# GpSimd waits for gathered rows at every second tile: one core, four graph layers

## The chip, the cores and the metric

The kernel runs on one core of a Trainium2 chip. The metric is the device time of one execution in microseconds, as the median of several runs.

## The reference

Four graph layers follow one another on x (4096 x 128) with one adjacency matrix adj (4096 x 4096, zeros and ones). Before each, x is normalised and floored at zero; the layer's result is added to x. The change lies in the last layer, which is this, cut to its core:

```
z  = leaky_relu(lap_mul(A, h) @ W1 + b1, 0.1)
d2 = sq[:, None] + sq[None, :] - 2.0 * (z @ z.T)
S  = exp(-sqrt(max(d2, 0) + 1e-10) / 2)
S  = where(ranks < 4, S, 0.0)          # the four nearest of each row
A2 = S + A
out = lap_mul(A2, h) @ W2 + b2         # lap_mul(A, x) = d * (A @ (d * x)), d = 1 / sqrt(rowsum(A))
```

So the last product is that of a dense 4096 x 4096 matrix of zeros and ones, plus, for each row, four rows of the same operand with four weights.

## The kernel before

The 4096 rows are 32 tiles of 128 (t), in 8 groups (g) of 4 (q). The kernel is written engine by engine; each engine goes through its list in order and waits on semaphores that count up. A wait holds everything behind it on its engine.

The last stage computes `A2 @ (d * x)` and the output. These are its parts.

TensorE: a tile's product (`product`, L684; matmuls at L680) is 32 matmuls of 128 x 128 weights (the transposed adjacency in 8 bits, tile `panel`, one of four slots q) against 384 bf16 columns (`partsB`), into bank q. It waits for the slot's panel (L687) and for the take of the product four tiles earlier, which frees the bank (L688). The first group is done by `first_products` (L694), all four products side by side. The matmuls of a product follow each other; the last one counts up `s_lprod`.

SP: `load_panel` (L438) loads the slot q of the next group, 512 KB, when the product of that slot is done (L500).

GpSimd: for each tile four gathers (`last_gathers`, L1406, DMA at L1413). One gather is an indirect DMA that fetches 128 rows of 512 bytes from DRAM (`last_features`) by the 128 indices of one column, so 64 KB. Tile t's gathers wait for the take of tile t - 3 (L1408). They land in `near[r * 4 + q]` (in the tile `gath`), with r the parity of the group: eight buffers, each with a semaphore of its own, `s_gath2`. At the third tile of a group the indices of the next group are copied first (`stage_near`, L1402), when the group before is used up (L1421). From the third group on, the buffer of tile t must have been used by tile t - 8 (L1424).

VectorE: `last` (L2193). For each tile it takes the product out of its bank (`take_product`, L1535, a sum over three parts into `agg`, counted by `s_sum`), waits for the tile's four gathers (L2202), and adds the four gathered rows with their weights (three operations at L2204, one at L2207, which counts up `s_gath_used`). After the fourth tile three operations make the output of the group (L2210, L2212, L2216).

ScalarE's queue: it stores each group's output, 256 KB.

An earlier stage, the pooling of the first layer, gathers too: GpSimd issues five gathers for each tile at L1324 and, at the second and fourth tile of a group, waits before them until those of the tile before have landed (`rows_landed`, L1312).

Of the kernel before, what the change touches and what calls it, by code (L numbers as in the profile page):

```python
# [26 lines left out]
G = 4  # L27
# [6 lines left out]
TOP = 4  # L34
# [18 lines left out]
def program(nc, x, adj, w0, b0, w1, w2, w31, b31, w32, b32, out):  # L53
    N, F = x.shape
    NT = N // P
    NG = NT // G
# [5 lines left out]
    with ctx:  # L62
# [3 lines left out]
        def sem(name):  # L66
            return ctx.enter_context(nc.semaphore(name))
# [197 lines left out]
        s_gath2 = [sem(f"nearest_gathered{i}") for i in range(2 * G)]  # L265
# [890 lines left out]
        def _(pool):  # L1156
# [245 lines left out]
            def stage_near(g, r):  # L1402

                pool.tensor_copy(near_idx[r], TI[:, ds(g * G, G), :].rearrange("p q k -> p (q k)")).then_inc(s_idx, 1)

            def last_gathers(g, r, q):  # L1406
                t = g * G + q
                pool.wait_ge(s_sum, 2 * NT + t + 2)  # L1408
                if q == 0:
                    pool.wait_ge(s_idx, NT + g + 1)  # L1410
                pool.sem_inc(waited["pool"], 1)
                for k in range(TOP):
                    pool.indirect_dma_start(near[r * G + q][:, k, :], None, g2_dram,  # L1413
                                            bass.IndirectOffsetOnAxis(near_idx[r][:, q * TOP + k:q * TOP + k + 1], axis=0)
                                            ).then_inc(s_gath2[r * G + q], 16)

            def last_group(g, r, first_pair=False, last=False):
                for q in range(G):
                    if q == 2 and not last:
                        if not (first_pair and r == 0):  # L1420
                            pool.wait_ge(s_gath_used, NT + g * G + 4)  # L1421
                        stage_near(g + 1, 1 - r)
                    if not first_pair:
                        pool.wait_ge(s_gath_used, NT + (g - 2) * G + q + 1 + 4)  # L1424
                    last_gathers(g, r, q)

            stage_near(0, 0)
            last_group(0, 0, True)
            last_group(1, 1, True)
            with pool.Fori(1, NG // 2 - 1) as h:  # L1430
                last_group(2 * h, 0)
                last_group(2 * h + 1, 1)
            pool.wait_ge(s_topi, 2 * NG)
            last_group(NG - 2, 0)
            last_group(NG - 1, 1, last=True)


        @block.vector
# [805 lines left out]
```

## Time and profile before

| what | us |
|---|---|
| time, median of 3 runs | 1810.25 |
| lowest and highest run | 1807.11 and 1820.14 |
| the profiled execution, span | 1795.6 |
| TensorE matmul busy, of the span | 1575.9 |
| GpSimd busy | 570.1 |
| L1413, the 128 gathers of the last stage, GpSimd | 124.4 |

The span reaches from the first to the last instruction of one execution, under the profiler. Engines are PE (TensorE matmul), PEld (its weight loads), DVE (VectorE), ACT (ScalarE), POOL (GpSimd) and SP. A gather's busy time on POOL is that of its issue; the transfer follows. PEclk is the granted TensorE clock as a share of the full one: 1.00 stands for 2.4 GHz and 0.50 for 1.2 GHz. Idle time is that of the engine just before an instruction, with what ended it; "issue" is a wait for nothing that the profile shows, "remote" a release by nothing that it can name. The last stage starts at about 1560 us and goes to the end.

### The profile page before, as it was taken

What the parts mean: (1) busy time and instruction counts of PE and PEld (TensorE: products, weight loads), DVE (VectorE), ACT (ScalarE), POOL (GpSimd) and SP (SyncE); (2) the same over time, 40 slices, a digit from 0 to 9 for tenths busy, and PEclk for the clock granted to TensorE, in tenths of its full rate; (3) what the DMA queues carried; (4) which work ended last, traced back from release to release, by engine and by line L of the source; (5) the groups of instructions that cost most, each with busy time, mean ns of one, the idle gap of its engine ahead of it and who ended that gap; (6) DMA issues with size and microseconds to landing.
All of it is one profiled execution on the core that took longest, in us unless ns stands there. A gap on an engine that the chain in (4) does not pass through costs nothing.

```text
span 1795.6 us, 32579 instructions
## 1 busy us (share of the span) xinstructions
PE 1575.9 (88%) x9161; PEld 926.1 (52%) x9161; DVE 1259.3 (70%) x3487; ACT 704.1 (39%) x1113; POOL 570.1 (32%) x813
## 2 busy tenths in 40 slices
PE   4999999866777777799998999999999999868987
PEld 3777777522333333356664666678544444434544
DVE  6799999855777677636556666642599999934344
ACT  3444444333444444213333222666455655500000
POOL 4333333356655555301111000233000000165663
PEclk9999999978888888899998999999999999988999
DMA  7687877423323222132222222444100000034442
GB/s 235 225 306 285 298 287 287 162 73 88 94 85 89 82 89 89 58 106 93 93 82 72 92 91 84 123 129 123 36 0 6 9 8 6 12 98 134 128 134 73
DMA packets 127159, 205.04 MB, mean 114 GB/s; under 512 B 11440, under 2 KB 95536, under 8 KB 118912
## 3 DMA queue, kind: packets, MB, share of 16 engines
q1 hardware_dynamic: 102592, 172.58, 28.3%
q0 software_dynamic: 11840, 25.52, 4.8%
q10 hardware_dynamic: 12672, 6.29, 1.2%
q8 instruction: 25, 0.41, 0.1%
q14 instruction: 30, 0.25, 0.0%
HBM read 178.13 MB, written 26.21 MB: 114 GB/s over the span
## 4 chain that ended last, share of the span: by engine, by line
PE 65%; DVE 13%; issue 11%; another core or an unknown queue 4%; ACT 3%; DMA 1%; SPq 1%; POOL 0%; DVEq 0%; ACTq 0%; POOLq 0%
PE bank L680 27%; PE bank L605 9%; PE bank L566 7%; PE bank L750 6%; DVE partsA L2131 5%; PE bank L594 4%; PE bank L817 3%; DVE cand L1605 3%; PE bank L571 2%; PE bank L529 2%; PE bank L542 2%; ACT first L918 1%; PE bank L818 1%; PE bank L519 1%
## 5 line engine op out<-in xcount | busy, mean ns | idle before, releaser
L680 PE MATMUL bank<-partsB,panel 128*128 128x387 bf16 (+1 forms) x2048 | 364.0, 336 | 48.1 <-issue 35.5
L680 PEld LDWEIGHTS bank<-partsB,panel 128*128 128x128 fp8e4 x2048 | 203.5, 100 | 204.2 <-issue 64.9
L817 PE MATMUL bank<-wide,partsA 128*128 128x512 f32 x512 | 263.3, 596 | 6.4 <-ACT rows L1122 4.9
L918 ACT ACTIVATE first<-bank 128x512 fp8e4<-128x512 f32 x256 | 150.2, 597 | 229.9 <-PE bank L594 92.2
L605 PE MATMUL bank<-first,partsB 128*128 128x512 fp8e4 x768 | 234.2, 419 | 6.3 <-DVE gath L1741 5.4
L1745 DVE TENSOR_TENSOR gath<-gath,bank 128x512 f32<-128x512 f32 x240 | 162.8, 682 | 98.5 <-PE bank L605 48.6
L1605 DVE MAX8 cand<-bank 128x8 f32<-128x128 f32 x1024 | 216.2, 281 | 10.4 <-PE bank L571 7.8
L566 PE MATMUL bank<-partsA,panel 128*128 128x387 bf16 x1024 | 212.0, 329 | 7.5 <-DVE cand L1605 6.1
L594 PE MATMUL bank<-panel,tri 128*128 128x512 fp8e4 x256 | 108.5, 425 | 101.3 <-ACT first L918 77.6
L872 ACT ACTIVATE panel<-bank 128x1024 fp8e4<-128x1024 bf16 x128 | 130.9, 1024 | 149.8 <-PE bank L542 149.8
L1324 POOL DMA_INDIRECT gath<-pool_features,idx_now x160 | 157.2, 983 | 85.5 <-issue 66.0
L1539 DVE TENSOR_REDUCE agg<-bank 128x128 f32<-128x384 f32 (+1 forms) x96 | 51.1, 555 | 187.8 <-PE bank L680 107.9
L1122 ACT COPY rows<-bank 128x512 f32<-128x512 f32 x256 | 133.1, 614 | 115.1 <-DVE partsA L2144 86.3
L680 PE MATMUL bank<-partsA,panel 128*128 128x384 bf16 x1024 | 172.4, 327 | 3.4 <-DVE gath L1745 1.7
L1193 POOL TENSOR_TENSOR rem<-gsc,partsB 128x516 f32<-128x516 f32 x23 | 26.0, 1130 | 452.6 <-ACT partsB L852 452.6
L817 PEld LDWEIGHTS bank<-wide,partsA 128*128 128x128 f32 x512 | 95.7, 190 | 103.2 <-ACT rows L1122 55.6
L1413 POOL DMA_INDIRECT gath<-last_features,IDX x128 | 124.4, 972 | 68.4 <-issue 47.7
L680 PEld LDWEIGHTS bank<-partsA,panel 128*128 128x128 fp8e4 x1024 | 99.6, 97 | 71.8 <-DVE gath L1745 2.2
L605 PEld LDWEIGHTS bank<-first,partsB 128*128 128x128 bf16 x768 | 80.1, 106 | 103.5 <-issue 41.6
L2131 DVE MAX8 partsA<-rows 128x8 f32<-128x4096 f32 x28 | 123.6, 4414 | 6.2 <-ACT rows L1122 6.2
L2144 DVE FIND_INDEX8 partsA<-partsA,rows 128x8 uint32<-128x4096 f32 x28 | 123.7, 4419 | 0.3 <-issue 0.3
L566 PEld LDWEIGHTS bank<-partsA,panel 128*128 128x128 fp8e4 x1024 | 89.2, 98 | 45.1 <-issue 10.6
(296 smaller groups left out, 2126.8 us busy)
## 6 DMA issues: line engine op xcount, KB each, us to landing
rows<-in_adj SPq DMA_DIRECT2D x64, 1024.0 KB, 7.0
panel<-adjT_panels SPq DMA_DIRECT2D x96, 512.0 KB
panel<-adjT_panels SPq DMA_DIRECT2D x128, 256.0 KB
adjT_panels<-panel SPq DMA_DIRECT2D x32, 512.0 KB, 3.0
gath<-pool_features,idx_now POOLq DMA_INDIRECT x160
overflow_maxima<-wide POOLq DMA_DIRECT2D x1, 2048.0 KB, 20.6
pool_features<-gsc ACTq DMA_DIRECT2D x8, 256.0 KB, 2.3
rows<-overflow_maxima SPq DMA_DIRECT2D x8, 256.0 KB
```

The lines of the kernel that those rows point to most:

```text
L566: i = pe.matmul(bank[q % 2][:, 0:FW], panel[:, q, j, :], parts_of[0][:, j, :], start=(j == 0), stop=(j == NT - 1))
L594: pe.matmul(tri_bank[j % 2][:, :], tri[:, :], piece[:, j // BPB, :, ts(j % BPB, P)], start=True, stop=True).then_inc(s_tri, 1)
L605: i = pe.matmul(pool_bank[j % 4][:, :], pparts[:, j, k * FE:k * FE + F], first_slot[:, j % SLOTS, :], start=(k == 0), stop=(k == 2))
L680: i = pe.matmul(bank[q][:, 0:3 * w], panel[:, q, j, :], of_block if w < FE else parts_of[u][:, j, :], start=(j == 0), stop=(j == NT - 1))
L817: pe.matmul(o[:, :], zs[:, q % 2, :], zT[:, c * 512:(c + 1) * 512], start=True, stop=False)
L872: act.activation(panel[:, q, c * 8:(c + 1) * 8, :].rearrange("p b i -> p (b i)"), bank[2 + c % 2][:, :].bitcast(BF16), ACT.Copy, saturate= ...
L918: act.activation(first_slot[:, j % SLOTS, :], tri_bank[j % 2][:, :], ACT.Relu, saturate=False).then_inc(s_first, 1)
L1122: act.copy(rows[:, q % 2, c * 512:(c + 1) * 512], bank[c][:, :]).then_inc(s_keyrow, 1)
L1324: pool.indirect_dma_start(main[q][:, k, :], None, feat_dram, bass.IndirectOffsetOnAxis(idx_now[:, q, k:k + 1], axis=0)).then_inc(s_gath[q] ...
L1605: i = dve.max(cand[:, ch * BPB + b, :], bank[4 + ch % 4][:, b * P:(b + 1) * P])
L1745: dve.tensor_tensor(running[:, j % 2, :], running[:, j % 2, :], pool_bank[j % 4][:, :], ALU.max).then_inc(s_fp_used, 1)
L2131: dve.max(top_v[:, q, :], rows[:, q % 2, :]).then_inc(s_top, 1)
```

## The change

Before the gathers of the third tile of a group (q == 2), GpSimd waits until the rows gathered for the second tile have landed. Before those of the first tile (q == 0), it waits until the rows gathered for the fourth tile of the group before have landed; the very first tile has no such wait. `h` counts pairs of groups and gives the value to wait for; `last_group` gets it as a new argument.

```diff
-            def last_group(g, r, first_pair=False, last=False):
+            def nearest_landed(h, r, q):
+
+                pool.wait_ge(s_gath2[r * G + q], 16 * TOP * (h + 1))
+
+            def last_group(g, h, r, first_pair=False, last=False):
                 for q in range(G):
+                    if q == 2:
+                        nearest_landed(h, r, 1)
+                    if q == 0 and r == 1:
+                        nearest_landed(h, 0, 3)
+                    if q == 0 and r == 0 and not first_pair:
+                        nearest_landed(h - 1, 1, 3)
                     if q == 2 and not last:
...
-            last_group(0, 0, True)
-            last_group(1, 1, True)
+            last_group(0, 0, 0, True)
+            last_group(1, 0, 1, True)
             with pool.Fori(1, NG // 2 - 1) as h:
-                last_group(2 * h, 0)
-                last_group(2 * h + 1, 1)
+                last_group(2 * h, h, 0)
+                last_group(2 * h + 1, h, 1)
             pool.wait_ge(s_topi, 2 * NG)
-            last_group(NG - 2, 0)
-            last_group(NG - 1, 1, last=True)
+            last_group(NG - 2, NG // 2 - 1, 0)
+            last_group(NG - 1, NG // 2 - 1, 1, last=True)
```

## Rows read from the trace of the kernel before

**Rows 1.** The page: span, and a group of instructions (busy, mean ns | idle)

```profile
span 1795.6 us, 32579 instructions
...
L1413 POOL DMA_INDIRECT gath<-last_features,IDX x128 | 124.4, 972 | 68.4 <-issue 47.7
```

**Rows 2.** Waits from 1579 us on: total us, times, longest

```profile
DVE agg L1539 <- remote: 71.3, 10, 12.5
...
POOL gath L1413 <- DVE agg L1539: 19.9, 6, 4.0
```

**Rows 3.** Windows: us, busy (xcount) of PE, PEld, DVE, ACT, POOL, PEclk, DMA, GB/s

```profile
1631.60:1636.90 5.30, 5.30 (x34) 3.12 (x32) 4.42 (x9) 0.00 (x0) 4.24 (x5) 1.00 0.46 148
...
1638.34:1642.95 4.61, 1.46 (x5) 0.50 (x6) 0.00 (x0) 0.00 (x0) 2.83 (x3) 0.96 0.22 59
1642.95:1647.72 4.77, 4.77 (x21) 2.45 (x21) 1.96 (x5) 0.00 (x0) 1.93 (x3) 0.68 0.39 125
...
1670.03:1675.04 5.01, 1.77 (x7) 0.70 (x8) 0.00 (x0) 0.00 (x0) 2.51 (x3) 0.83 0.18 52
...
1767.88:1771.24 3.36, 0.65 (x3) 0.11 (x2) 0.00 (x0) 0.00 (x0) 1.22 (x2) 1.00 0.42 117
1597.30:1619.30 22.00, 4.80 (x13) 1.22 (x12) 6.06 (x14) 0.00 (x0) 13.94 (x16) 0.60 0.21 60
```

**Rows 4.** Timeline of TensorE, last stage: start us, us, instructions [idle before]

```profile
1586.72 10.58 PE L680 MATMUL bank<-partsB,panel 128*128 128x384 bf16 x53 [2.91 <-DMA panel<-adjT_panels]
...
1619.30 19.04 PE L680 MATMUL bank<-partsB,panel 128*128 128x384 bf16 x104 [0.90 <-issue]
...
1642.95 27.07 PE L680 MATMUL bank<-partsB,panel 128*128 128x384 bf16 x153 [1.08 <-issue]
```

**Rows 5.** Timeline of GpSimd, last stage

```profile
1579.95 0.99 POOL L1413 DMA_INDIRECT gath<-last_features,IDX  x1 [0.82 <-POOL IDX L1404]
...
1593.93 0.95 POOL L1413 DMA_INDIRECT gath<-last_features,IDX  x1 [0.30 <-issue]
...
1619.34 0.95 POOL L1413 DMA_INDIRECT gath<-last_features,IDX  x1 [3.97 <-DVE agg L1539]
...
1657.88 0.94 POOL L1413 DMA_INDIRECT gath<-last_features,IDX  x1 [2.99 <-DVE agg L1539]
...
1676.66 0.95 POOL L1413 DMA_INDIRECT gath<-last_features,IDX  x1 [3.50 <-DVE agg L1539]
...
1755.64 0.95 POOL L1413 DMA_INDIRECT gath<-last_features,IDX  x1 [1.56 <-issue]
```

**Rows 6.** Timeline of VectorE, last stage

```profile
1589.93 1.13 DVE L2204 SCALAR_TENSOR_TENSOR agg<-gath,sg,agg 128x128 f32<-128x128 f32 x3 [7.43 <-DMA gath<-last_features,IDX]
...
1596.49 1.13 DVE L2204 SCALAR_TENSOR_TENSOR agg<-gath,sg,agg 128x128 f32<-128x128 f32 x3 [2.56 <-DMA gath<-last_features,IDX]
...
1617.97 0.56 DVE L1539 TENSOR_REDUCE agg<-bank 128x128 f32<-128x384 f32 x1 [12.45 <-remote]
...
1665.13 0.56 DVE L1539 TENSOR_REDUCE agg<-bank 128x128 f32<-128x384 f32 x1 [1.48 <-PE bank L680]
...
1675.22 0.56 DVE L1539 TENSOR_REDUCE agg<-bank 128x128 f32<-128x384 f32 x1 [7.90 <-remote]
...
1788.15 0.56 DVE L1539 TENSOR_REDUCE agg<-bank 128x128 f32<-128x384 f32 x1 [3.19 <-PE bank L680]
...
1791.95 0.69 DVE L2216 TENSOR_TENSOR partsA<-X,tmp 128x512 f32<-128x512 f32 x1
```

**Rows 7.** Pooling stage: GpSimd's waits, 359 to 745 us, and its timeline

```profile
POOL gath L1324 <- DMA gath<-pool_features,idx_now: 17.0, 7, 3.1
...
404.79 0.95 POOL L1324 DMA_INDIRECT gath<-pool_features,idx_now  x1 [2.38 <-issue]
```

**Rows 8.** Pooling stage, TensorE: timeline, and window (busy, PEclk, DMA, GB/s)

```profile
418.40 0.59 PE L594 MATMUL bank<-panel,tri 128*128 128x512 fp8e4 x1 [4.56 <-ACT first L918]
...
359.00:745.00 386.00, 279.42 (x1217) 0.84 0.29 85
```

## Prediction

> **What bounds the kernel now.** I read the page first. The span is 1795.6 us and the last stage holds the 128 gathers of L1413, 124.4 us of GpSimd [rows 1]. Then, for the stretch from 1579 us on, the waits, then each engine's timeline. The waits look odd: VectorE sat 71.3 us before its take of a product (L1539) for a releaser that the profile cannot name, and GpSimd waited only 19.9 us for VectorE [rows 2].
>
> TensorE's timeline tells what that is. A product is 32 matmuls; at full rate those take 5.30 us (1631.60 to 1636.90, granted clock 1.00) [rows 3]. The 28 products of groups 1 to 7 run from 1586.72 [rows 4] to 1788.15, when the take of the last starts [rows 6]: 201.4 us. 28 x 5.30 is 148.4 us, so 53 us are lost, and not to missing work. In 22.00 us from 1597.30 TensorE ran 13 matmuls; in 4.61 us from 1638.34, 5; in 5.01 us from 1670.03, 7 [rows 3]. There are seven such stretches, the other four of 3.4 to 5.0 us. After some, the clock is granted at half for a while (0.68 on the mean in the 4.77 us after the second) [rows 3].
>
> What else happens then? GpSimd's timeline gives the answer I build on. The gathers of a tile are four, 1.25 us from start to start, and two tiles follow each other with a gap of 0.30 us unless a wait stops them. A run without a pause begins at 1657.88, and TensorE goes slow at 1670.03, 12.1 us later; another begins at 1755.64, and it goes slow at 1767.88, 12.2 us later [rows 3, 5]. In the first run (from 1579.95, with little TensorE work at its start) it took 17 us. Runs of eight gathers or fewer have no slow stretch; the longest of them is that from 1645.18 to 1654.9, before the pause of 2.99 us [rows 5]. TensorE leaves a stretch 1.1 to 3.9 us after the run's last gather is out: the first at 1619.30 [rows 4], where the next gather starts at 1619.34 after 3.97 us of idleness [rows 5].
>
> VectorE sees it too, and earlier. The first product of group 1 has had its 32 matmuls by about 1593.8 (14 of them at the half clock that the gap before 1586.72 had brought), yet its take starts at 1617.97, after 12.45 us of waiting; the take at 1675.22 waited 7.90 us [rows 6] for a product whose last matmul lies eight before 1670.02, the end of 153 that ran unbroken [rows 4], so it was done at about 1668.9. TensorE's completions are held back while gathers follow one another and come about 1.6 us after the last one is out. The same shows in the pooling stage, where ten gathers and a store ran from 404.79 to 418.5 without a pause: TensorE sat 4.56 us and started again at 418.40 [rows 7, 8]. So the bound of this stage is TensorE, kept slow by long unbroken runs of gathers. I have no mechanism for it, only its timing.
>
> **The change, part by part.** It removes nothing, moves no copy and no DMA. It adds 15 waits on GpSimd: before tiles 2, 4, ... 30 of the 32 (counted from 0), each for the four gathers of the tile just before. Behind the waiting instruction are queued the index copy (L1404, at the third tile of a group), then the gathers of that tile and all later ones; VectorE waits for them at L2202. SP's panel loads and the output stores on ScalarE's queue do not stand behind GpSimd.
>
> *Price of one wait.* The last stage shows none, but the pooling stage has the same construction, five gathers and then a wait until they landed. Its start at 404.79 came 2.38 us after the end of the gather before, and 7 such waits that the profile names sum to 17.0 us, 2.43 each, longest 3.1 [rows 7]. The last stage agrees from its own rows: the gather issued from 1593.93 on (out by 1594.88) lets VectorE start at 1596.49, 1.61 us after [rows 5, 6], and a GpSimd gather starts some 0.8 us after what it waited for: together 2.4. I take 2.43, with 2.24 (the shortest in the pooling stage) and 3.1 as ends. When panel loads fill the DMA engines a landing is later: the first tile's rows came 5.2 us after their last issue (take of 1589.93) [rows 6]. A copy in the pause adds 0.2 us of work, but the copy of the index starts sooner after a release than a gather does; I add nothing for it.
>
> The Trainium skill (page "DMA: Bandwidth & Descriptors", section "Anatomy of one DMA — SWDGE (gpsimd) path") puts one DMA at 2.0 us plus its bytes over 436 GB/s, 2.15 us for 64 KB. By that estimate, and the same 0.8 us to start again, the pause would be 2.0 us and the time 1791; the trace has 2.56 us from the start of the issue to the landing, so I go by the trace.
>
> *Does the wait lie on the path?* GpSimd is now idle often, since a tile's gathers wait for the take three tiles back (L1408). Four of the fifteen places have a pause of 2.6 us or more already (1676.66, with 3.50 us, is one) [rows 5]; there the wait would be free today. But if the slow stretches go, the takes are early and GpSimd is no longer held by them: then every wait counts, and GpSimd paces the stage. Check that nothing else does: TensorE needs 10.6 us for two products; a product waits for the take four tiles back, which needs the rows five tiles back, landed long before; panel loads are issued a group ahead.
>
> *The new sum.* Eight gathers: 7 x 1.25 + 0.95 = 9.70 us. Longer issues: 124.4 us for 128 against 0.947 each is 3.2 us in all, 0.2 a pair. Pause 2.43. A pair of tiles costs 12.33 us, more than TensorE's 10.6. The first pair starts at 1579.95 as before [rows 5]; the sixteenth starts 15 x 12.33 = 185.0 us later, at 1764.9, where the last gather is out at 1774.6. It lands 1.6 us later, 1776.2; four multiply-adds take 1.5 us, 1777.7; the last three operations of the group take 2.4 us (1790.3 to 1792.64) [rows 6]: 1780.1. Before it was 1792.64: 12.5 us earlier.
>
> So two large terms nearly cancel: TensorE gets back some 53 us, and GpSimd, which without waits would end at 1579.95 + 128 x 1.25 + 3.2 + 1.4 for seven copies + 1.6 + 1.5 + 2.4 = 1750, is made 30 us longer by the waits. What is left is 12.5 us. Against the profiled execution 1795.6 - 12.5 = 1783.1 us; the median stands 14.65 us above that execution's span, so 1810.25 - 12.5 = 1797.8. I say 1798.
>
> **Rivals.**
>
> *A. The forecast*, GpSimd paces, 1798. Its own range: with 2.24 us a pause and no long issues, 5.9 us better, 1792; with 3.1, 10 us worse, 1808.
>
> *B. The stretches stay.* Their cause may be the number of gathers in some longer window, and 2.4 us may not clear what has built up. For it: completions are already late after 7 to 8 us of a run (the take at 1665.13 came late though its run began at 1657.88), and a run of eight is 10 us. Against: a pause of 1.56 us before 1755.64 was followed by a full 12.2 us of good TensorE [rows 5]; and in the pooling stage, with pauses of 2.4 us every five or ten gathers, completions move again after each. If they stay at their size, TensorE paces as now and 11 of the 15 waits are put where there is no pause today; GpSimd's 11 x 2.1 = 23 us go into the 35 us that it now waits for takes (68.4 us idle before gathers [rows 1] less some 110 ordinary gaps of 0.30). Time 1805 to 1815, say 1810.
>
> The Trainium skill (page "SBUF — State Buffer", section "SBUF: two separate sides") says that a DMA and a compute engine's access do not slow each other. By that rule the gathers are not what holds TensorE, the stretches have another cause, and this case B is what comes. The trace has seven stretches in step with gather runs, which speaks against it.
>
> *C. Slower: the stretches are the profiler's.* TensorE issues the most instructions, so if recording them were what chokes, the unprofiled kernel would have no stretches, and the waits would only cost. Then the time before is set by GpSimd, ending at 1750, and after at 1780: 30 us more, 1840. It decides if the unprofiled stage is shorter than the profiled by more than about 12 us. Against it: the profiled span would be 42 us too long, and the median would hold 57 us outside of the kernel instead of 14.65. The spread of the runs (1807 to 1820) also suits a stall of varying length.
>
> The Trainium skill (page "Runtime: NRT & Kernel Launch", section "The ~15µs preamble/postamble breakdown") gives 9 to 15 us around a kernel, which fits 14.65 and not 57; by that page C falls.
>
> *D. More is gained.* Landing 1.25 us after the last issue and 0.8 us to start make a pause of 2.05, and no long issues: 5.7 + 3 us better than A, 1789. Or the unprofiled stretches are longer than the profiled ones. Against that stands TensorE's clock, since it would now idle 1.7 us in every 12.3: at the 0.84 that it was granted in the pooling stage, where it idles more [rows 8], 10.6 us become 12.6, about the pair's own time; that is 0 to 5 us within A's upper end.
>
> **Chances.** A 0.63, B 0.17, C 0.09, D 0.11. The time is A's. Range 1788 to 1813: it takes in D's figure, all of A and B's middle, and leaves out C, B's upper end and the far part of D. Over 1% faster (about what a measurement of this kernel tells from no change) means under 1792.1: D and the best of A, 0.25. Over 1% slower, above 1828.4: C and a bad B, 0.12. The rest, 0.63, within 1%.
>
> **What the profile after would show.** Right: no matmul gaps over 1 us in a stretch of several; all products from the second group on in about 5.3 us, with short idle times between; VectorE's idle time before L2204 for the gathers, not before L1539 for "remote"; GpSimd's gathers in runs of eight with pauses of 2.3 to 2.6 us, 15 of them named or "issue"; the last gather issued near 1774. Wrong: stretches of 0.7 us and more from matmul to matmul that remain (B); pauses over 3 us (the price of a wait); the span much shorter and the median not (C); TensorE's clock at half over whole products (the pace would be TensorE's).

## The result, and the profile after

On the first chip the changed kernel takes 1803.38 us (median of 16 runs, 1797.04 to 1810.85) and the kernel before 1813.42 us (16 runs, 1802.66 to 1824.11). The ratio is 0.9951 with a 95% interval of 0.9935 to 0.9967: 0.5% faster, some 9 us, inside the 1% that I had called no change. I had said 1798 and a gain of 12.5 us.

The spans alone say the opposite. The page of the changed kernel, its first line and three of its costliest groups (columns as in [rows 1]):

```profile
span 1805.4 us, 32578 instructions
...
L918 ACT ACTIVATE first<-bank 128x512 fp8e4<-128x512 f32 x256 | 150.1, 597 | 250.0 <-remote 106.6
...
L1413 POOL DMA_INDIRECT gath<-last_features,IDX x128 | 123.9, 968 | 60.4 <-issue 56.7
...
L2214 DVE SCALAR_TENSOR_TENSOR agg<-gath,sg,agg 128x128 f32<-128x128 f32 x96 | 34.0, 354 | 113.8 <-DMA gath<-last_features,IDX 111.4
```

1805.4 us is 9.8 us longer than the span before [rows 1]. Before reading that as a loss, look at where the last stage starts: its first gather stands at 1599.02 (below), before at 1579.95 [rows 5]. So 19.1 us were lost ahead of the change, in code that it doesn't touch. The pooling stage, from the first to the last matmul of L605, takes 415.9 us here and 396.1 us before. That difference, and not the change, decides the comparison of the two spans. Where it comes from can't be settled: the profiled execution of before would have taken 1797.3 us (its span and the 1.7 us told below), less than each of the 16 runs of the kernel before that stand beside the changed one (1802.66 and more), so it may well be from another chip or moment than these. I therefore measure the last stage by itself in every profile, from the start of the first gather to the end of VectorE's last operation: before 1579.95 to 1792.64 [rows 5, 6], 212.7 us; after 1599.02 to 1802.45, 203.4 us. The stage is 9.3 us shorter, which is about what the medians say; on chip 2, where both kernels were profiled, it is 3.4 us (e5 and e6 below), of single executions 3.2 us apart in time, and the medians there are 8.3 us apart.

The waits of the changed kernel from 1599 us on (as [rows 2]: engine, tile, line, what it waited for, total us, times, longest):

```profile
DVE agg L2214 <- DMA gath<-last_features,IDX: 111.4, 32, 6.8
...
POOL IDX L1404 <- DMA gath<-last_features,IDX: 13.0, 7, 2.7
PE bank L680 <- issue: 10.6, 8, 2.8
PE bank L680 <- DVE agg L1549: 6.5, 5, 2.2
...
POOL gath L1413 <- DMA gath<-last_features,IDX: 2.3, 1, 2.3
```

In [rows 2] VectorE waited 71.3 us before its take of a product for something that the profile cannot name, and GpSimd waited for VectorE. The first row is gone, and of the second 0.6 us are left. VectorE now waits before each tile for its rows, 111.4 us in all: GpSimd sets the pace. TensorE and GpSimd from the start of the stage (timelines: start us, us, instructions, [idle before]):

```profile
1607.17 38.89 PE L680 MATMUL bank<-partsB,panel 128*128 128x384 bf16 x224 [2.79 <-issue]
1646.28 5.46 PE L680 MATMUL bank<-partsB,panel 128*128 128x384 bf16 x32 [0.22 <-DVE agg L1549]
1653.29 5.46 PE L680 MATMUL bank<-partsB,panel 128*128 128x384 bf16 x32 [1.55 <-DVE agg L1549]
...
1703.52 23.00 PE L680 MATMUL bank<-partsB,panel 128*128 128x384 bf16 x128 [2.17 <-DVE agg L1549]
```

```profile
1599.02 0.99 POOL L1413 DMA_INDIRECT gath<-last_features,IDX  x1 [0.81 <-POOL IDX L1404]
...
1611.49 0.20 POOL L1404 COPY IDX<-partsA 128x16 int32<-128x16 int32 x1 [2.74 <-DMA gath<-last_features,IDX]
1612.24 0.97 POOL L1413 DMA_INDIRECT gath<-last_features,IDX  x1 [0.56 <-issue]
...
1624.24 0.94 POOL L1413 DMA_INDIRECT gath<-last_features,IDX  x1 [2.28 <-issue]
...
1648.90 0.97 POOL L1413 DMA_INDIRECT gath<-last_features,IDX  x1 [2.61 <-issue]
...
1776.20 1.37 POOL L1413 DMA_INDIRECT gath<-last_features,IDX  x1 [1.69 <-issue]
```

Seven products (224 matmuls) run in 38.89 us without a gap, where before 13 matmuls filled 22 us [rows 3, 4]. After that TensorE stops only at product boundaries, for a buffer that VectorE has yet to empty. GpSimd goes in runs of eight gathers with a pause of 2.3 to 2.7 us between (3.49 us the first).

A word on times and spans: each run of the study has a span beside its time, and the time is 1.7 us longer, give or take 0.1 (in the profiled run here 1807.13 and 1805.4). The prediction had taken 14.65 us for what lies around the kernel; see below.

### The profile page after: what moved, and what is told of

Same layout as the page of the kernel before. It is cut to its first block and busy times, and to the rows that moved or that the text cites. A ratio compares the mean times of both kernels' runs of the same rounds, so it can differ in the third digit from the quotient of the medians.

```text
span 1805.4 us, 32578 instructions
## 1 busy us (share of the span) xinstructions
PE 1574.1 (87%) x9151; PEld 926.1 (51%) x9161; DVE 1260.4 (70%) x3487; ACT 704.1 (39%) x1113; POOL 568.0 (31%) x813
## 5 line engine op out<-in xcount | busy, mean ns | idle before, releaser
L680 PE MATMUL bank<-partsB,panel 128*128 128x387 bf16 (+1 forms) x2048 | 353.2, 332 | 27.4 <-issue 10.7
L605 PE MATMUL bank<-first,partsB 128*128 128x512 fp8e4 x768 | 239.7, 427 | 5.6 <-DVE gath L1751 5.4
L594 PE MATMUL bank<-panel,tri 128*128 128x512 fp8e4 x256 | 110.0, 431 | 114.7 <-ACT first L918 91.5
L1413 POOL DMA_INDIRECT gath<-last_features,IDX x128 | 123.9, 968 | 60.4 <-issue 56.7
L680 PEld LDWEIGHTS bank<-partsA,panel 128*128 128x128 fp8e4 x1024 | 99.6, 97 | 71.7 <-DVE gath L1755 2.2
L605 PEld LDWEIGHTS bank<-first,partsB 128*128 128x128 bf16 x768 | 80.8, 107 | 103.9 <-issue 43.6
L594 PEld LDWEIGHTS bank<-panel,tri 128*128 128x128 bf16 x256 | 26.9, 105 | 176.0 <-issue 157.6
L2214 DVE SCALAR_TENSOR_TENSOR agg<-gath,sg,agg 128x128 f32<-128x128 f32 x96 | 34.0, 354 | 113.8 <-DMA gath<-last_features,IDX 111.4
```

Of the source, the lines that this page charges most:

```text
L594: pe.matmul(tri_bank[j % 2][:, :], tri[:, :], piece[:, j // BPB, :, ts(j % BPB, P)], start=True, stop=True).then_inc(s_tri, 1)
L605: i = pe.matmul(pool_bank[j % 4][:, :], pparts[:, j, k * FE:k * FE + F], first_slot[:, j % SLOTS, :], start=(k == 0), stop=(k == 2))
L680: i = pe.matmul(bank[q][:, 0:3 * w], panel[:, q, j, :], of_block if w < FE else parts_of[u][:, j, :], start=(j == 0), stop=(j == NT - 1))
```

## The experiments

The runs fell on four further chips, numbered 2, 5, 9 and 13; the first chip is that of the result above. Kernels of one chip share its runs of the kernel before, and only such times are compared. Each of these chips was met in one session only, so "chip" stands below for a chip and its moment; the runs don't separate the two. Two numbers come from each profile: the length of the last stage as above, and the **excess**, which is what the 28 products of groups 1 to 7 took, over 5.30 us each (from the start of a product's first matmul to the start of its last, and 0.17 us for that one): 51.6 us in the profile of before, 3.2 us in that of after.

**e1_earlier_tile, e3_three_of_four, e4_pool_pause, on chip 5.** First, what if GpSimd waits for rows that have long landed (e1), or for three of the last four gathers (e3); and what does the same cure do in the pooling stage (e4)? (e2, a first form of e7 below, gave no result.)

e1, every wait one tile earlier:

```
-    nearest_landed(h, r, 1)
+    nearest_landed(h, r, 0)
...
-    nearest_landed(h, 0, 3)
+    nearest_landed(h, 0, 2)
...
-    nearest_landed(h - 1, 1, 3)
+    nearest_landed(h - 1, 1, 2)
```

> The changed kernel with each of the 15 waits on the tile one further back (three tiles' semaphores later it would be the same place in the program, but those rows have landed by then), so the waits are there and cost nothing, and gathers follow each other as before. If it is the pause in the gathers that keeps TensorE at its rate: the slow stretches return, last stage about 213 us from first gather to end, time as the kernel before (ratio 1.00). If the mere bound on gathers in flight or the changed order of instructions does it: stage 203 us or less, no stretches, faster than before by over 0.5%.

e3, the fourth gather of tiles 1 and 3 counts on another semaphore, which VectorE waits for as well:

```
-    ).then_inc(s_gath2[r * G + q], 16)
+    ).then_inc(s_gath[2 * r + q // 2] if q % 2 and k >= 3 else s_gath2[r * G + q], 16)
...
-    pool.wait_ge(s_gath2[r * G + q], 16 * TOP * (h + 1))
+    pool.wait_ge(s_gath2[r * G + q], 16 * 3 * (h + 1))
...
```

> The changed kernel with each of the 15 waits for three of the four gathers of the tile before (the fourth counts on another semaphore), so that a pause is one gather shorter, about 1.3 us for 2.6. If a pause of 1.3 us clears what has built up: no slow stretch, a pair of tiles costs 11.3 us, the last stage is 15 x 1.25 = 19 us shorter than the changed kernel's 203.4, about 185, and the time about 1784 (ratio to before 0.985). If 1.3 us does not clear it: slow stretches come back after a few pairs, stage 195 to 215 us.

e4, the changed kernel and one wait more in each turn of the pooling stage:

```
     store_overflow(g)
+    rows_landed(g, 3)
```

> The changed kernel with one more wait in the pooling stage: at the end of each group GpSimd waits until the rows of its fourth tile have landed, so that its gathers come in runs of five where ten and a store followed one another. If held-back completions of TensorE slow the pooling stage in the same way: its idle time for 'remote' at L918 falls from 107 us by a third or more, the stage (396 and 416 us in the two profiles) gets 10 to 30 us shorter and the scatter of the runs falls. If the pooling stage is bound by the pace of its own chain: no change within 3 us, or some 5 us slower.

The kernel before ran there in 1708.0 us (13 runs, 1705.41 to 1713.62), a hundred microseconds less than on the first chip. e1 took 1709.12 us, ratio 1.0007 (0.9996 to 1.0018); e3 1726.46, 1.0107 (1.009 to 1.0123); e4 1751.33, 1.0252 (1.0234 to 1.0269). TensorE's timeline of e1 for the whole of groups 1 to 7, and the window in the middle of it (columns as [rows 3]):

```profile
1544.59 149.82 PE L680 MATMUL bank<-partsB,panel 128*128 128x384 bf16 x896 [2.79 <-DMA panel<-adjT_panels]
...
1600.00:1690.00 90.00, 90.00 (x546) 52.97 (x544) 44.17 (x106) 0.00 (x0) 69.23 (x74) 1.00 0.51 153
```

896 matmuls, all 28 products, in one piece, in the window shown at the full clock, while 128 gathers ran with no gap over 0.47 us. Every completion of a product was seen within 0.1 us. So there is nothing on this chip to cure: the stretches are no property of the kernel alone. The last stage takes 169.0 us in e1, 187.7 in e3 and 211.4 in e4. What e1 would do where there are stretches was not tried. Nor was e4's wait in the pooling stage tried there, so whether it would help that stage stays open. e4's pauses are the longest of all, up to 3.8 us after the first; why isn't shown. Its first pause is

```profile
1551.56 0.19 POOL L1405 COPY IDX<-partsA 128x16 int32<-128x16 int32 x1 [4.20 <-DMA gath<-last_features,IDX]
```

**e5_before_traced, e6_change_again, e7_pause_only, on chip 2.** Was chip 5 or the first one the exception? e5 is the kernel before, e6 the changed one. e7 has the 15 pauses but waits for no rows: GpSimd fills a tile that nobody reads any more with zeros at those places.

```
-    pool.wait_ge(s_gath2[r * G + q], 16 * TOP * (h + 1))
+    pool.wait_ge(s_prefix, 1 + 2 * (2 * h + r) + q // 2)
+    pool.sem_inc(waited["pool"], 1)
+    pool.memset(zT[:, 0:2304], 0.0).then_inc(s_prefix, 1)
```

Each fill waits for the fill before it, which has long ended.

> The kernel before itself, for its trace on the chip of this call. The runs of before took 1813 us on the first chip and 1708 us on that of the experiments so far. If the held-back completions of TensorE are a matter of the chip (or of what runs beside it): where the time is near 1708 us, no stretches and every completion seen within 0.1 us, the last stage some 169 us from the first gather to the end for 213; where it is near 1813, the stretches again.

> The changed kernel itself. Where the kernel before has stretches (time near 1813 us): ratio 0.995 again. Where it has none (time near 1708 us), the waits only cost: the last stage 203 us as on the first chip against 169, so some 34 us slower, ratio 1.020; with the sum of the prediction (12.33 us a pair) 30 us, 1.018.

> The changed kernel with each of the 15 waits replaced by one write of zeros by GpSimd (128 x 2304, about 2 us) to a tile that is no longer read, so GpSimd pauses about as long, but no landing is waited for. Where the kernel before has stretches: if a pause in GpSimd's issue is enough, none here and the stage 200 to 206 us; if it must be the landing, stretches and 208 us or more. Where it has none: the pause costs what it lasts, stage 200 us, ratio 1.018, as the waits do.

The kernel before took 1793.49 us there (12 runs, 1782.38 to 1798.31). e5, one execution, 1794.34. e6 1785.15, ratio 0.9956 (0.9936 to 0.9976). e7 1778.99, ratio 0.9912 (0.988 to 0.9943): the lowest ratio that I have. The windows from 1600 to 1690 us of e5, e6 and e7, in this order (columns as [rows 3]):

```profile
1600.00:1690.00 90.00, 68.08 (x351) 35.46 (x351) 31.57 (x76) 0.00 (x0) 55.32 (x60) 0.83 0.38 115
```

```profile
1600.00:1690.00 90.00, 79.65 (x464) 45.11 (x463) 35.83 (x86) 0.00 (x0) 56.82 (x61) 0.98 0.47 142
```

```profile
1600.00:1690.00 90.00, 83.02 (x487) 47.28 (x485) 37.95 (x91) 0.00 (x0) 73.01 (x71) 0.98 0.47 144
```

351 matmuls in 90 us before, 464 with the change, 487 with the bare pauses, 546 on chip 5. The excess is 48.1, 3.1 and 1.6 us. In e5 VectorE waits for what the profile can't name again, as in [rows 2]:

```profile
DVE agg L1539 <- remote: 68.0, 10, 14.0
```

In e7 the waits for rows are replaced by this (GpSimd's timeline):

```profile
1586.11 2.03 POOL L1421 MEMSET wide<- 128x2304 f32 x1
1588.08 0.20 POOL L1404 COPY IDX<-partsA 128x16 int32<-128x16 int32 x1
1588.45 0.98 POOL L1413 DMA_INDIRECT gath<-last_features,IDX  x1 [0.17 <-POOL IDX L1404]
```

That is 2.33 us from the end of one gather to the start of the next, and 2.2 without a copy. The stretches are gone all the same, so it is the pause in issuing that cures, and not that the rows have landed. The last stage is 205.9 us in e6 and 199.6 in e7. The gaps of over 0.45 us between gathers sum to 42.5 and 33.9 us, 8.6 apart; e7's issues are 2.0 us longer in all (126.0 against 124.0), and the rest is back in the 6.3 us between the stages.

**e8_earlier_tile_b, e9_three_of_four_b, e10_pause_short, e11_pause_both, on chip 9.** e8 and e9 are e1 and e3 again. e10 is e7 with a shorter fill, e11 is e7 with the wait in the pooling stage that e4 has.

```
-    pool.memset(zT[:, 0:2304], 0.0).then_inc(s_prefix, 1)
+    pool.memset(zT[:, 0:1000], 0.0).then_inc(s_prefix, 1)
```

> The kernel of e1_earlier_tile once more (each wait on rows that have landed by then, so it makes no pause), for a chip on which the kernel before has stretches. If the pause keeps TensorE at its rate: stretches as in the kernel before, the products of groups 1 to 7 some 50 us over 28 x 5.3, last stage 211 to 216 us, ratio 1.00. If a wait alone did it: no stretches. On a chip without stretches: ratio 1.00 either way.

> The kernel of e3_three_of_four once more (waits for three of the four gathers, pause about 1.3 us). On a chip with stretches: if 1.3 us is enough, no stretch, stage 190 us as on the chip without, some 18 us less than the change's 209, ratio 0.986; if not, stretches return in part and the stage is 195 to 215 us. On a chip without: ratio 1.011 again.

> The kernel of e7_pause_only with the write of zeros cut from 2304 to 1000 columns, so a pause of about 1.15 us instead of 2.27. On a chip with stretches: if such a pause is enough, no stretch and the stage 15 x 1.1 = 17 us shorter than its 202.5, 186, ratio 0.982; if it is the length of the pause that clears what has built up, stretches return in part, stage 190 to 212. On a chip without: stage 186, ratio 1.009.

> The kernel of e7_pause_only and, in the pooling stage, a wait at the end of each group until the rows of its fourth tile have landed, which breaks its run of ten gathers and a store. On a chip with stretches the pooling stage took 397 us in e7_pause_only and 348 on the chip without: if held-back completions in that run cost the difference, it gets 10 to 30 us shorter, ratio 0.97 to 0.985; if not, within 4 us of 0.991. On a chip without: pooling some 4 us longer (352 for 348 in e4), ratio 1.02.

I had hoped for a chip with stretches; this was another without. Before 1709.41 us (13 runs, 1704.96 to 1712.04). e8 1711.94, ratio 1.0017 (1.0003 to 1.0032; one of its eight runs took 4828.99 us, for no reason on record, and is not in the ratio). e9 1727.71, 1.0101 (1.0084 to 1.0119). e10 1724.64, 1.0093 (1.0076 to 1.0111). e11 1741.39, 1.0186 (1.0169 to 1.0203). As tests of the cure they say nothing. As prices of a pause they are the cleanest numbers of the study, because here GpSimd paces the stage in each of them. The pauses are the gaps of over 0.45 us between gathers: 15 in e10 and e11, 16 in e9, e3 and e4. Each replaces an ordinary gap of 0.30, so 4.5 or 4.8 us are taken off. The stage without pauses is e1's 169.0 us on chip 5 and e8's 170.0 on chip 9:

| | chip | pauses less ordinary gaps | last stage over that without pauses | time over the kernel before |
|---|---|---|---|---|
| e10 | 9 | 13.1 us | 12.1 us | 15.2 us |
| e3 | 5 | 19.7 us | 18.7 us | 18.5 us |
| e9 | 9 | 20.9 us | 19.1 us | 18.3 us |
| e11 | 9 | 29.4 us | 28.9 us | 32.0 us |
| e4 | 5 | 43.6 us | 42.4 us | 43.3 us |

A microsecond of pause costs a microsecond, within 2 us for the stage. e11's pooling stage, with its extra wait, takes 349.2 us and e4's 352.0; without it e1's takes 348.5 and e10's 351.9. Without held-back completions the wait there costs next to nothing, and the 43 us of e4 are in the last stage.

**e12_pause_short_b, e13_change_b, on chip 13.** Is a pause of 1.15 us enough? e12 is e10 again, e13 the changed kernel.

> The kernel of e10_pause_short once more. On a chip on which the kernel before has stretches (time 1780 us or more): if a pause of 1.15 us after every eight gathers is enough, no stretch, stage 186 us, ratio 0.982; if the length of the pause counts, stretches return in part, stage 190 to 212 us. On a chip without: ratio 1.009 again.

> The changed kernel itself. On a chip with stretches: ratio 0.995 and a stage of 204 to 209 us, as before. On a chip without, where it has not run yet: no stretch to remove, the waits only cost; the kernel with the waits of which only three of four gathers count took 1.010, a pause here is one gather longer, 15 x 1.25 = 19 us more, so ratio 1.021, stage 209 us.

This chip has the stretches. Before 1793.34 us (19 runs, 1786.95 to 1801.02); e12 1788.20, ratio 0.9975 (0.9955 to 0.9995); e13 1788.37, 0.9963 (0.9938 to 0.9987). The times are alike and the profiles aren't. TensorE in e12, from its timeline, and the window of e12:

```profile
1596.46 0.32 PE L680 MATMUL bank<-partsB,panel 128*128 128x384 bf16 x1 [0.41 <-issue]
1597.85 0.33 PE L680 MATMUL bank<-partsB,panel 128*128 128x384 bf16 x1 [1.07 <-issue]
...
1624.06 16.15 PE L680 MATMUL bank<-partsB,panel 128*128 128x384 bf16 x90 [0.27 <-issue]
...
1600.00:1690.00 90.00, 73.49 (x376) 36.47 (x376) 34.74 (x79) 0.00 (x0) 63.52 (x69) 0.87 0.42 125
```

The pauses of 1.11 and 1.25 us let a stretch of over 27 us come (1596.5 to 1624.1), and the excess is 40.6 us, where e13 has 4.4. What e12 loses to stretches it saves in pauses: last stage 204.7 us, e13 203.8. e12 also shows that it isn't the added instructions that cure: they are those of e7, and only the length of the fill differs (on another chip than e7's).

## Why the prediction was right, and where it was not

**The bound, and that the pauses lift it: right.** Excess 51.6 us in the profile of before and 3.2 in that of after; 48.1 and 3.1 on one and the same chip, 2. No stretch is left, and e7 shows that the regularity which I read off [rows 3, 5] (no stretch in a run of eight gathers) is cause and not company: only the pause was added there. TensorE's completions are still held back after the change, by up to 3.6 us where an update can be told (5 of the 32 are missing from the trace), but only two of the 28 products took longer than 5.3 us, 6.9 each. Both came after a stop of over 2 us (idle 2.79 and 2.17 us), and over the second, 1703.52 to 1710.60, the granted clock was 0.76 on the mean.

**GpSimd paces: right**, by VectorE's 111.4 us of waiting for rows, and by the table above. The prediction's sum for GpSimd without waits, 1579.95 to 1750, is 170.1 us; e1 has 169.0 and e8 170.0. And with pauses of 2.2 us the last stage takes 199.6 us on a chip with stretches (e7) and 198.9 us on one without (e11). So once the stretches are gone, the chips are alike in this stage.

**The sum: 3.3 us short.** Forecast 1579.95 to 1780.1, 200.15 us; measured 203.4. The 15 pauses sum to 38.6 us, 2.57 each, where I took 2.43: 2.1 us. The first was 3.49 (the copy's wait of 2.74, the copy 0.20, and 0.56 until the gather); I had put a copy at nothing. One gap more, of 1.69 us at 1776.20, is no wait of the change. The kernel before has it too, as 1.56 at 1755.64 [rows 5], and I had read it as a pause of the pace without counting it: 1.4 us over an ordinary gap. Long issues were 0.5 us less than in the sum (123.9 us in all). That makes 3.0 of the 3.3. The gain by stage is 9.3 us instead of 12.5. The time, 1803.38, is 5.4 us over the 1798 that I said; 3.2 of these are that the kernel before, too, has a higher median in 16 runs (1813.42) than in the three that I counted from (1810.25).

**14.65 us around the kernel: wrong.** I took median less span for a constant and used it twice. It is 1.7 us in each run. The other 13 us were that the profiled execution of before was faster than the three runs shown, by its pooling stage if the profile of after is a guide: 396.1 us against 415.9, where chips 2 and 13 have 392.6 to 400.3. The forecast came out near all the same, since it is the median of before less 12.5 us: what I had taken off to come from the median to the span was added again at the end. The argument against rival C hung on it and was void. The Trainium skill (page "Runtime: NRT & Kernel Launch", section "The ~15µs preamble/postamble breakdown") had fitted my wrong reading; the 1.7 us leave no room for 9 to 15 between this time and this span.

**Rival C: its price is real, its reason isn't shown and isn't excluded.** It said: without stretches the waits only cost, 30 us. On chips 5 and 9 that is what pauses do: e11, whose pauses of 2.2 us are shorter than those of the change, has a last stage 28.9 us over e8's. From the table the change alone would cost there 38.6 - 4.5 = 34 us, 2%, an estimate; it was not run there by itself. But C blamed the profiler. Chips 5 and 9 were profiled like the others and show no stretch, so recording alone doesn't make them. Yet the profiles differ in one more thing. Where there are stretches, records are missing too. The last stage's gathers among the DMA issues of e5 and of e1 (the last number is the median us from issue to landing):

```profile
gath<-last_features,IDX POOLq DMA_INDIRECT x128
```

```profile
gath<-last_features,IDX POOLq DMA_INDIRECT x128, 2.7
```

e5 has no time to landing, since most updates that tell of one are not in its trace. The 164 DMAs of the stage should leave 16 updates each, 2624. By the end of VectorE's work e1 has 2604 of them, e5 654, the profile of before 673, that of after 819. Outside of the two stages with gathers e5 misses hardly any: ahead of the pooling stage it has 2018 updates of DMAs, e1 2016. So stretches and lost records come on the same chips, in the same stages; the last stages of e12 and e13 have 695 and 913 of the 2624, that of e10 2586. Whether the load of recording holds TensorE there, or one cause makes both, no run here can tell, nor whether the stretches would be there if nothing were recorded, since every run lists spans and clocks. The 0.4 to 0.9% that pauses gain may hold only under recording.

**Rival B: did not come, but it was nearer than I argued.** My evidence against it was a pause of 1.56 us followed by 12 us of good TensorE [rows 5]. e12 shows that pauses of 1.1 to 1.25 us every eight gathers leave an excess of 40.6 us beside the 48.1 and 51.6 of the kernel before on two other chips (on chip 13 itself the kernel before was not profiled). So something of an earlier run is carried over a short pause, as B said; 2.2 us clear enough of it. Where between 1.25 and 2.2 us it turns was not tried.

**Rival D** was not reached by the change. e7 comes nearer with its shorter pauses, without reaching it: 0.9912, where D's 1789 is 0.988 of 1810.25.

## What to carry to other kernels

When a matmul stream breaks up, or an engine waits for something that the trace can't name, lay the GpSimd timeline beside it: if the breaks follow long unbroken runs of indirect gathers, some 2 us of pause after eight of them is worth a trial, made of plain work rather than of a wait for the rows. Such a pause costs its full length where GpSimd paces and the chip has no such breaks (here 0.9 to 2.5% lost on two chips, with pauses of 1.1 us and more; 0.4 to 0.9% won on three, with pauses of 2.2 us and more), so measure on several chips before you keep it. Look too whether the profile has lost records in that stage (no time to landing in its DMA issues): then compare times without the profiler, if you can. And compare stages, not spans, of two single executions, and read time less span within one and the same run before you build on it.

## What the runs showed of the hardware that I had not expected

**The same program on different chips.** Before: 1813.42, 1793.49 and 1793.34 us on the first chip, 2 and 13; 1708.0 and 1709.41 on 5 and 9. Of the 84 to 105 us between the kinds, some 40 to 44 lie in the last stage (209.3 us in e5 and 212.7 in the profile of before, against 169.0 of e1, which stands for the kernel before since its time is within 0.1%), and 41 to 67 in the pooling stage (392.6 to 415.9 us against 348.5 to 352.0, over all profiles). In the waits of ScalarE in the pooling stage, from 350 to 700 us, it looks like this in e5:

```profile
ACT first L918 <- remote: 88.5, 26, 6.5
```

and e1 has no such row there: 117.3 us, all named as waits for TensorE's L594. Outside of the two stages with gathers no completion comes over 0.1 us late in e5, whichever engine sends it. Within them, only TensorE's do: in the pooling stage 98 of its 393 updates on record are over 1 us late, up to 6.8, and in the last stage 14 of 27, up to 26.0. All of VectorE's (326 and 123) and ScalarE's (202) that are on record there come within 0.1 us, though about a third of their updates are missing. So what is slow on these chips, as far as the trace tells, is TensorE, in its completions and in its steps from matmul to matmul. What differs between the chips stays open.

**How late.** In e5 the completion of the first product of group 1 came 26.0 us after its last matmul, by the trace's semaphore updates, and VectorE's take followed it at once. (Where updates are missing, other single values are rough.)

The Trainium skill (page "SBUF — State Buffer", section "SBUF: two separate sides") says that DMA and compute engines do not slow each other there. On chips 5 and 9 the trace agrees, with 896 matmuls unbroken beside 128 gathers; on the first chip and chip 2 TensorE lost about 50 us in step with them. That doesn't contradict the page, since no run shows that SBUF is where it happens.
